# Two local-attention layers on one core: when the last unit's heads, the projections and the second layer's weights are worked

## The reference, cut to what matters

```
h = shift_token(x)                      # upper 128 channels come from the token before
q, k, v = split(h @ wqkv[l])            # 256 -> 3 x 512, 8 heads of 64
q, k = l2norm(q) * qs, l2norm(k) * ks;  q, k = rotary_xpos(q, k)
# windows of 128 queries over their own and the previous 128 keys, causal
o = softmax(8 * q k^T + mask) v
x = x + o @ wo[l]                       # 512 -> 256
h = layernorm(shift_token(x)) * g + b
a, g = split(h @ w1[l] + b1[l])         # 256 -> 2 x 682
x = x + (a * gelu(g)) @ w2[l] + b2[l]   # 682 -> 256
```

## Time and profile before

| | |
|---|---|
| median of three executions | 2286.31 us |
| the profiled execution's own time | 2285.73 us |
| its span, first to last instruction | 2283.9 us |
| mean granted TensorE clock over the span, as a share of full speed | 0.937 |
| busy share of the span: TensorE, VectorE, ScalarE, GpSimd | 83%, 65%, 52%, 44% |
| first `minima` of group 0 | 724.3 us |
| group 7 and group 8, first `minima` to the next group's first | 106.6 us, 123.7 us |

### The profile page before, as it was taken

One profiled execution on the slowest core, in us unless ns is written; L12 is line 12 of the kernel. 1 busy time (PEld: TensorE's weight loads), 2 busy tenths in 40 slices (PEclk: granted clock), 3 DMA queues, 4 the chain that ended last, 5 costly groups with the idle time before them and its releaser, 6 DMA issues.

```text
span 2283.9 us, 36427 instructions
## 1 busy us (share of the span) xinstructions
PE 1890.0 (83%) x12941; PEld 1414.6 (62%) x12941; DVE 1474.4 (65%) x3723; ACT 1185.1 (52%) x2717; POOL 995.1 (44%) x788
## 2 busy tenths in 40 slices
PE   4569999998926888898898887876888888888897
PEld 3444444444424777677776776765776777767776
DVE  3678887777446576575765765564665757657574
ACT  0545555343514564655656556563646556465563
POOL 0314555466725444343434435442534445444451
PEclk6779999999957999999999998998999999999998
DMA  4000010101131000000000002010001000010000
GB/s 136 25 24 27 1 33 16 45 18 49 36 110 49 16 20 10 28 15 16 20 17 21 15 16 63 15 57 25 24 15 32 22 26 24 17 32 20 28 17 22
DMA packets 83406, 68.58 MB, mean 30 GB/s; under 512 B 10852, under 2 KB 79508, under 8 KB 83224
## 3 DMA queue, kind: packets, MB, share of 16 engines
q1 hardware_dynamic: 83224, 66.25, 9.4%
HBM read 45.22 MB, written 16.81 MB: 27 GB/s over the span
## 4 chain that ended last, share of the span: by engine, by line
PE 36%; DVE 15%; ACT 7%; issue 6%; DMA 5%; POOL 1%; SPq 1%; DVEq 0%; ACTq 0%; POOLq 0%
PE bank_P L259 5%; PE bank_P L261 4%; PE bank_P L260 4%; PE bank_T L1187 4%; DMA l_xs<-l_xs 4%; PE bank_O L1199 4%; PE bank_A L1176 3%; PE bank_T L1166 2%; PE bank_A L259 2%; PE bank_A L261 2%; PE bank_A L260 2%; ACT l_sm L1332 2%; DVE l_sm L1515 2%; DVE l_ra L88 1%; ACT l_pt L1341 1%
## 5 line engine op out<-in xcount | busy, mean ns | idle before, releaser
L1706 POOL TENSOR_TENSOR l_sm<-l_sm,l_rinv 128x512 f32<-128x512 f32 (+1 forms) x256 | 249.5, 994 | 290.6 <-DVE l_rinv L1523 290.6
L1694 POOL TENSOR_TENSOR l_t<-l_qk,l_tab 128x512 f32<-128x512 f32 x128 | 170.2, 1351 | 359.8 <-DVE l_ss L1482 309.7
L1332 ACT ACTIVATE l_sm<-l_sm,l_nb 128x256 f32<-128x256 f32 (+1 forms) x512 | 247.9, 486 | 96.7 <-DVE l_nb L1515 96.2
L259 PE MATMUL bank_P<-l_wqkv_hi,l_h_hi 128*128 128x512 f32 x384 | 165.0, 430 | 85.3 <-ACT l_qk L1304 40.4
L259 PE MATMUL bank_A<-l_f_hi,l_w_hi 128*114 128x256 f32 (+1 forms) x768 | 221.2, 288 | 4.3 <-DVE l_f_lo L1556 3.7
L260 PE MATMUL bank_A<-l_f_lo,l_w_hi 128*114 128x256 f32 (+1 forms) x768 | 216.8, 282 | 0.0
L261 PE MATMUL bank_A<-l_f_hi,l_w_lo 128*114 128x256 f32 (+1 forms) x768 | 216.8, 282 | 0.0
L1515 DVE CUSTOM_DVE_ANT_0 l_sm<-bank_A,l_mask 128x256 f32<-128x256 f32 (+1 forms) x512 | 177.2, 402 | 57.2 <-PE bank_A L1176 56.9
L617 ACT ACTIVATE pr<-ps_S 128x1024 f32<-128x1024 f32 x128 | 130.7, 1023 | 122.9 <-PE ps_S L511 122.2
L1187 PE MATMUL bank_T<-ident,l_sm 128*128 128x128 f32 x960 | 139.8, 286 | 58.3 <-POOL l_sm L1706 57.9
L1341 ACT COPY l_pt<-bank_T 128x512 f32<-128x512 f32 (+1 forms) x256 | 130.3, 560 | 108.4 <-PE bank_T L1187 54.2
(11 more groups left out here) (242 smaller groups left out, 5111.0 us busy)
## 6 DMA issues: line engine op xcount, KB each, us to landing
l_xs<-x_layers SPq DMA_DIRECT2D x64, 128.0 KB, 2.5
x<-in_x SPq DMA_DIRECT2D x8, 512.0 KB, 3.9
base_rows<-x SPq DMA_DIRECT2D x16, 256.0 KB, 2.1
x_layers<-x SPq DMA_DIRECT2D x16, 256.0 KB, 2.2
l_xs<-x_layers SPq DMA_DIRECT2D x64, 64.0 KB, 2.1
x_layers<-l_yb SPq DMA_DIRECT2D x32, 128.0 KB, 1.8
l_base<-base_rows SPq DMA_DIRECT2D x32, 128.0 KB, 2.7
out<-l_yb SPq DMA_DIRECT2D x32, 128.0 KB, 1.7
```

The source lines that it names most:

```text
L259: pe.matmul(out, a_hi, b_hi, start=(start and k == 0), stop=False)
L1332: eng.activation(row, row, ACT.Exp, bias=nb[:, R % SS, e:e + 1], scale=-1.0, accum_out=rsum[:, R % SS, e:e + 1]).then_inc(ex_ready, 1)
L1694: eng.tensor_tensor(dst[:, :, :, lo:lo + H2], src[:, :, :, hi:hi + H2], table[:, :, 1, lo:lo + H2].unsqueeze(2).to_broadcast([P, 2, LH, H2 ...
L1706: eng.tensor_tensor(row, row, rinv[:, R % SS, :].unsqueeze(2).to_broadcast([P, 2, P * windows(n)]), ALU.mult).then_inc(pn_ready, 1)
```

## The change

Five things change, all in `layers_block`.

1. The rounds stretch ends after round 11 (`EARLY` = 12). The four rounds of the last unit are done in slots 0 and 1 (scores, two pairs per slot) and slots 0 to 3 (transposes and values); there are 16 slots, and hidden chunks, their outputs and everything that hangs on them stand one slot later.
2. The six left-over `outputs` stand in rounds 0 and 2, three each, and `y_out` in round 4; `qk_transpose` of the third and fourth unit in rounds 4 and 6 (they were in 4 and 10), with `rotated` in VectorE's rounds 3 and 5. `finish`, GpSimd's last work on a result, goes from round 9 to round 6.
3. `project` writes a T bank and no longer P. In the first fill (group -1) `qkv` goes round P, A0, A1 and A2.
4. One input transpose with its high and low part goes from round 14 to round 10, one to slot 1.
5. The pieces have four places: the first 512 columns of the tiles `ge`, `up`, `xn` and `base`. SP issues them in batches (4 + 2 in group 7; 4 + 4 + 3 in group 8); the wqkv pieces come ahead of `tables(1)`. The w2 pieces are worked in slot 0. `gelu`, `up_out` and `layer_norm` of groups 7 and 8 wait until the pieces that stand in their tiles are used.

```diff
+EARLY = ROUNDS - PAIRS
-SLOTS = HC + 3
+SLOTS = HC + 4
-        piece = base[:, :, :].rearrange("p a d -> p (a d)")
+        pieces = [a[:, 0:2, :].rearrange("p a d -> p (a d)") for a in (ge, up, xn, base)]
-        OUT_AT = {0: (0, 1), 2: (2, 3), 4: (4,), 6: (5,)}
-        W_Q = {1: 0, 3: 1, 5: 2, 7: 3, 9: 4, 11: 5}
-        W_O = {0: 0, 2: 1}
-        W_1 = {4: 0, 6: 1, 8: 2, 10: 3, 12: 4, 14: 5}
-        W_2 = {1: 0, 3: 1, 5: 2}
+        OUT_AT = {0: (0, 1, 2), 2: (3, 4, 5)}
+        W_Q = {2: (0, 1), 3: (2, 3), 8: (4, 5)}
+        W_O = {2: (0, 1)}
+        W_1 = {3: (0, 1), 7: (2, 3), 8: (4, 5)}
+        AT_Q = pieces + pieces[0:2]
+        AT_O, AT_1, AT_2 = pieces[0:2], pieces[2:4] + pieces, pieces[0:2] + pieces[3:4]
             def qkv(n, a):
-                ps = fill(w, kind, i, "P")
+                ps = fill(w, kind, i, "P" if n >= QUAD else ("P", "A0", "A1", "A2")[(3 * n + a) % 4])
             def project(n):
-                ps = fill(w, "wo", n, "P")
+                ps = fill(w, "wo", n, "T")
# TensorE, the slots
                 for k in range(SLOTS):
+                    r = EARLY + 2 * k
+                    if g >= 0 and k < 4:
+                        p_transpose(*head(first, r - 4)), p_transpose(*head(first, r - 3))
+                    if g >= 0 and k < 2:
+                        scores(*head(first, r)), scores(*head(first, r + 1))
                     if k < HC and ahead:
                         qkv(following + k // 3, k % 3)
                     if g >= 0:
-                        if k < 2:
-                            p_transpose(first + 3, 2 * k), p_transpose(first + 3, 2 * k + 1)
-                        if 1 <= k < 3:
-                            values(first + 3, 2 * k - 2), values(first + 3, 2 * k - 1)
-                        if k in (1, 5):
-                            project(first + 2 + k // 4)
-                        if k == 2:
+                        if k in (0, 4, 6):
+                            project(first + (1, 0, 2, 3)[k // 2])
+                        if k == 3:
                             x_transpose(first), x_transpose(first + 1)
+                        if k < 4:
+                            values(*head(first, r - 4)), values(*head(first, r - 3))
+                    if k in ((1, 4, 7) if g >= 0 else (4, 7)) and ahead:
+                        h_transpose(following + 1 + k // 3)
-                    if k >= 3 and g >= 0:
-                        hidden(m0 + k - 3)
+                    if k >= 4 and g >= 0:
+                        hidden(m0 + k - 4)
...
# ScalarE, the slots: o_out at k = 0, 2, 4; pt_out; qkv_out(k); then
+                        if k < 2:
+                            exps(*head(first, r)), exps(*head(first, r + 1))
+                        if g == GL and k == 0:
+                            piece_2(0), piece_2(1), piece_2(2)
+                        if k == 3:
+                            f_out(first), f_out(first + 1)
+                    if k in ((1, 4, 7) if g >= 0 else (4, 7)) and ahead:
+                        h_out(following + 1 + k // 3)
...
# VectorE, the slots
+                        if k < 3:
+                            inverse(*head(first, r - 2)), inverse(*head(first, r - 1))
+                        if k in (0, 2, 4):
+                            o_split(first + 1 + k // 2)
+                        if k < 2:
+                            minima(*head(first, r)), minima(*head(first, r + 1))
                         if k == 0:
-                            o_split(first + 2)
-                            inverse(first + 3, 2), inverse(first + 3, 3)
+                            residual(first + 1)
+                            moments(first)
+                        if k == 1:
+                            if ahead:
+                                h_split(following + 1)
                             moments(first + 1)
                             deviation(first // 2)
+                        if k == 2:
                             layer_norm(first // 2, rs)
...
# SP
+            def take_q():
+                w.wait_ge(u_ready, HC * (GL - 1))
+                filled(w, "x_t", UL - QUAD - 1)
+                for i in range(6):
+                    if i == 4:
+                        w.wait_ge(wq_ready, KC + 2)
+                    k, s = divmod(i, 3)
+                    take(AT_Q[i], io["wqkv"][1, P * k:P * k + P, 512 * s:512 * s + 512])
+            def take_rest():
+                w.wait_ge(u_ready, HC * GL)
+                filled(w, "x_t", UL - 1)
+                w.wait_ge(wq_ready, KC + 6)
+                ...                                  # wo 0, 1 and w1 0, 1
+                w.wait_ge(wo_ready, 3)
+                w.wait_ge(w1_ready, KC + 2)
+                ...                                  # w1 2 to 5
+                w.wait_ge(w1_ready, KC + 6)
+                ...                                  # w2 0, 1, 2
```

266 lines of the change are left out of this document (129 added, 137 removed).

## The result

The changed kernel takes 2208.94 us (median; 2207.61 to 2215.19), the kernel before in the same comparison 2290.9: a ratio of 0.9649 [0.9614, 0.9684], 3.5% faster. The forecast was 2229 with a range of 2195 to 2270, so the time lies in it, on the fast side. On the profiled executions, against which the sum was made, it is 2285.73 to 2207.61: 78 us where 57 were forecast.

The account below looks back on a forecast made before the run. TensorE, busy 83% of 2283.9 us, was taken as the bound. Ordinary groups -30, group 7 -4, group 8 -18, first fill -2 and last group -3 sum to -57: 2285.7 to 2229 us, range 2195 to 2270.

Parts of the forecast that it names:

- second rival: Whole kernel: no chain is late, 4.5 us per ordinary group go, 30 for the rest, 2198 us; chance 14%.
- ordinary groups: Groups 0 to 6 and 9 to 14: -2.3 us for each of 13 with the clock, -30 us in all.
- A: First 12 rounds of group 5, 26.4 us: outputs fill a wait, y_out moves, T banks cost; net -1.1 us.
- C: Group 5 after the first hidden chunk, 43.8 us: bank P wait goes, second layer norm wait stays; -0.6 us.
- the clock: TensorE's granted clock in ordinary groups: filled wait may gain 1.3 us, new slot waits may cost 1.7; taken as +0.2.
- The wait of 0.68 us at bank P goes: Rest of an ordinary group, ahead of the fourth unit's project: the wait ends because project takes a free T bank.
- the P waits ... go: First slots: interleaving puts 3 us or more between qkv products, ending bank P waits of 1.22, 1.25 and a shorter one.
- B: Last unit's rounds and slots to the first hidden chunk: 4.3 us of waits for 4.7; 25.7 to 24.9 us, -0.8.
- Group 7: First weight batch ahead of the table, ScalarE waits 3.5 us; excess over an ordinary group 8 instead of 12, -4 us.
- group 8: The 13.19 us wait for w2 goes, new copies cost 3, clock and small waits help: about -18 us.
- no wait, or 1 to 2 us: Group 8, slot 0: three w2 pieces, requested in round 9 and worked 6 us or more later, hardly delay ScalarE.
- Ends: First fill: qkv no longer waits for bank P, -2 us; last group: interleaved rounds and slots, unchanged tail, -3 us.

Follow-up runs that it names:

- the first experiment: The kernel before with only the four piece places, batches and w2 pieces in slot 0 changed: 2275.11 us, ratio 0.992.
- the two last experiments: Changed kernel with earlier input transpose, VectorE's new slot-1 order and the last group reordered: 2171.12 us; same plus SP's shift and load ahead of w2 in group 8: 2171.56.

## Why the prediction came out as it did

**Direction and size.** Right in direction, 21 us too careful in size. The time lies between the forecast and the second rival (*TensorE fills up*, 2198), and the ordinary groups, 4.1 us shorter, are nearer to that rival's 4.5 than to the forecast's 2.3. Against the rival stand the two waits in the slots: a chain is late, as the forecast had it. Of its signs three came: no TensorE wait over 6 us in groups 7 and 8 (5.50 is the longest), none at bank P behind ScalarE's copy in group 5, and the low part of h in slot 2. Two did not: ordinary groups are at 90.7 and 91.4 us on the mean, below the 92 to 94, and the wait ahead of slot 3 is VectorE's `o_split`, not GpSimd.

**Where the 21 us are.** In the ordinary groups, which gave 53.7 us for the 30 forecast. TensorE's waiting (length less busy time, and the windows after) went from 161.6 to 127.6 us there, 2.6 per group, where parts A to C had 2.5; its busy time fell by 1.5 per group for the same work, where the sum had +0.2 under the clock. Summed this way, the clock is the term that was mis-sized. But the parts of the waiting were off as well, and busy time and waiting trade with each other: the kernel of 2175 us and the one with the transpose alone have 23.9 and 10.2 us at 1.2 GHz in groups 9 to 14, and these windows:

```profile
1545.07:2079.56 534.49, 495.84 (x3770) 415.58 (x3770) 391.13 (x1099) 328.54 (x852) 265.58 (x240) 0.98 0.09 26
1550.90:2085.09 534.19, 490.39 (x3770) 411.88 (x3770) 391.05 (x1099) 328.44 (x852) 265.59 (x240) 0.99 0.09 26
```

The first has 5.5 us more of busy time and 5.2 us less of waiting, and the lengths are 0.3 us apart. So the account by waits does not tell what an edit is worth; the experiments do.

**Project and bank P: the credit that went to the wrong edits.** The prediction says of it "The wait of 0.68 us at bank P goes", with 0.7 under `y_out` against a loss of 0.6 at the T banks, and leaves the other waits there to the interleaving ("so the P waits ... go"). The runs say otherwise: `project` in T is worth 3.0 us a group alone, 2.9 and 3.2 inside the change; interleaving cures only the wait between two `qkv` (1.22), since a `project` stands straight behind a `qkv` in three slots. So by edit it is `project` 3.0 us where the sum had nothing (0.6 lost, 0.6 won), outputs and `y_out` 0.2 to 0.45 where it had 2.1, the rounds with their transposes 0.9 where it had 0.4. The error was in the walk: I took a list of waits and gave each to the edit that stood nearest, without asking in which pairs the second product follows the first in the same bank. That list was already whole in the profile of before: 1.25 + 0.52 + 0.68 + 0.67 = 3.1 us, of which only 1.25 and 0.68 stood in the earlier trace rows. All four were in the sum nevertheless, 1.25 and 0.52 of them in the 4.7 us of B, of which the prediction says that most stands between one `qkv` and the next (1.22 does). The error so gave the credit to the wrong edits and did not by itself make the sum short.

**A** (forecast -1.1): 26.4 to 25.1, -1.3, nearly as summed, but made up otherwise. The waits grew, from 2.8 to 3.3 us, and the busy time fell from 23.6 to 21.8, with the clock at 1.00 where it was 0.94. The first wait on GpSimd went from 1.66 to 0.96. In place of the 0.67 for `y_out` the first `project` waits 0.56 for `o_split`; the T banks cost 0.49 and 0.30, and `qk_transpose` in round 4, which TensorE reaches earlier now that the `outputs` of that round are gone, waits 0.65 for its input; the walk had left that out.

**B and C** (forecast -0.8 and -0.6): the windows give -0.5 and -2.9. One `qkv`, six products of 0.235 us or 1.4 us, has moved from C to B with the extra slot, so for the same work it is -1.9 and -1.5. "The gaps are traded, hardly removed" was too dark: B's waits went from 4.7 to 3.2 us where 4.3 were forecast. The low part of h holds TensorE 1.48 us for 2, and one wait of 1.73 stands for the 1.5, 0.5 and 0.3. C's went from 3.7 to 2.4: the 0.68 at bank P, 0.4 on the layer norm (1.40 to 0.97) and 0.2 ahead of it.

**The clock** (taken as +0.2, bounds -1.3 and +1.7): the granted clock went to the good end. Before, groups 2, 4 and 5 each have a stretch of 3.4 us at 1.2 GHz right behind the first wait on GpSimd (group 2 another one later), and groups 9 to 14 have 27.3 us of such stretches; after, groups 1 to 6 have none, with that wait at 0.96 us in group 5, and groups 9 to 14 have 10.2 us. The two new waits of 1.48 and 1.73 us, 2.3 us of work apart, brought none. With the outputs back where they were (542.5 against 541.4) stretches of 3.4 us return in every other group, for 0.2 us a group: the wait filled and the clock held are one and the same small gain.

**Groups 7 and 8.** Group 7: "Excess over an ordinary group: 8 instead of 12" is what came, 12.4 to 8.3 us (98.5 less the mean of groups 1 to 6). ScalarE waits 2.15 us for the first batch where 3.5 were forecast, and TensorE behind it

```profile
1369.02 1.97 PE L1168 MATMUL bank_T<-ident,l_t 128*128 128x128 f32 x8 [3.59 <-ACT l_pt L1346]
```

The sum left out that groups 7 and 8 are ordinary groups too and gain what these gain, 4 us each. So group 7 gave 8 rather than 4, and group 8's own gain is 11 rather than 18: 12.1 in the first experiment. There the rows are

```profile
1467.57 1.97 PE L1168 MATMUL bank_T<-ident,l_t 128*128 128x128 f32 x8 [5.21 <-ACT l_pt L1346]
...
1500.64 2.03 PE L1201 MATMUL bank_O<-l_pt,l_vt 128*64 128x128 f32 x16 [5.50 <-ACT l_pt L1346]
1505.39 0.69 PE L1150 MATMUL bank_T<-ident,l_xs 128*128 128x128 f32 x2 [2.72 <-DMA l_xs<-x_layers]
```

13.19 The earlier trace rows went, 5.50 came: "no wait, or 1 to 2 us" for w2 was wrong, ScalarE stood 6.90 us before that batch. The step that failed is the price of the transfer. The prediction put the long wait down to the place in SP's queue. That place only decided when it began: ScalarE's 14.74 us begin at 1566.38, SP issues at 1566.49, and the packets of the 113 rows run from 1570.94 to 1580.62, 9.7 us at 24 GB/s. The batch of the change has the same piece in it and takes 15.4 us, where the prediction had slot 0 "6 us or more later" and called that enough. "the loads are wanted in slot 1: covered" was wrong by 2.72, and 13.64 where the transpose stands a slot earlier, since SP could issue them only after it. The granted clock of the group is 0.89, not 0.98.

**Ends.** The first fill gave 3.9 us for 2, of which the longer part before it hides 1.8. The last group was to gain 3 and lost 1.1: it waits 4.15 us on `o_split` where 2.65 on GpSimd stood, and 6.01 on the layer norm, before 3.89. I had called the tail unchanged; the order of VectorE in it was not.

**Luck.** Two errors met: w2 and the loads of group 8 (some 7 us) and the last group (4) fell short, and the ordinary groups, with the ordinary share of groups 7 and 8, gave more than that back. That A came within 0.2 us of its sum is luck too: its waits were 2.0 us more than summed, its busy time 2.2 less.

**Four versions beat both kernels.** The changed kernel with the transpose one slot earlier makes 2177 us, 2175 with VectorE's order as well, and with the last group's order on top 2171 us (2172 with SP's order too), 5.2% below the kernel before (0.9477 [0.9451, 0.9502]); the intervals of the four overlap. TensorE is still at 86% there, and the two places left are the 13.64 us of group 8, behind the 113-row piece, and the last group.

## What to carry to other kernels

List the pairs of products that follow each other in one bank and charge each with the copy between them; filling the time with other work helps only if it stands between the two. Undo each part by itself before the named part of a change gets the credit: here one letter gave 3 us a group and the large move with its transposes 0.9. When a producer is moved on one in-order engine, look for its consumer on the others: `finish` ahead of `y_out` came with 4.2 us more in each group of layer 1, and a late low part of h cost two waits, one of them on an operation that has nothing to do with h. When a wait ends with a transfer, look at the transfer's own rate before its place in the queue is changed.

## What the runs showed of the hardware

**A piece of 113 rows.** 226 packets of 1 KB to 113 rows took 9.7 us (24 GB/s), 228 packets of 1 KB to 114 rows 2.3 us; what SP issued behind the first was slow as well, 8.98 us for two stores that take 0.82 elsewhere. The same slow stretch stands in group 8 of the changed kernel and of the two last experiments.

**Which waits the granted clock forgives.** In group 5 before, the wait of 1.66 us with one of 0.37 behind it was followed, 2 us later, by 3.4 us at 1.2 GHz. After, waits of 0.96 and 0.37 us there, and of 1.48 and 1.73 us in the slots, are followed by none. With VectorE's order alone changed, the 2.55 us wait that ends at 1218.24 is: the window right behind it shows

```profile
1218.20:1221.60 3.40, 3.36 (x10) 2.56 (x10) 1.94 (x3) 0.59 (x1) 1.79 (x2) 0.50 0.20 58
```

That kernel has such a stretch in four of its groups 1 to 6, the changed kernel in none, and so its shorter waits (2.55 for 1.48 + 1.73) bring no time. No single length of wait decides in these runs. Before, 1.66 us in group 5 and 1.45 in groups 2 and 4 were followed by such a stretch, 1.66 and 1.67 in groups 1 and 3 were not; after, 1.73 never was, and 2.03 us was in group 13 and was not in group 9.

**What a stretch at 1.2 GHz costs.** Little, where other engines hold TensorE in the same rounds anyway: 13.7 us more of it in six groups came with 0.3 us more of length (the two windows above), and 10.2 us more in six others with 1.1 us, the outputs having moved too. In the slots, where TensorE is full, it costs more: with VectorE's order alone changed, groups 1 to 6 have 13.7 us of it, wait 4.3 us less, are busy 5.5 us more and take 1.2 us longer.
